# Attention values in column halves, softmax sums by 32 columns of ones in column quarters

## The reference

```
q = (x @ Wq + bq).reshape(Bv, Tv, 16, 8)
k = (x @ Wk + bk).reshape(Bv, Tv, 16, 64)
v = (x @ Wv + bv).reshape(Bv, Tv, 16, 64)
qc = einsum('bthd,dl->bthl', q, Wc)
att = einsum('bthl,bshl->bhts', qc, k) / 8
att = softmax(where(causal, att, -inf), axis=-1)
y = einsum('bhts,bshl->bthl', att, v).reshape(Bv, Tv, 16 * 64)
return y @ Wo + bo
```

## Time and profile before

| | |
|---|---|
| median of 3 runs | 1122.53 us (1118.86 to 1125.27) |
| the profiled execution | 1125.98 us, span 1124.2 us |
| PE busy | 904.0 us, 80% of the span |
| DVE / ACT / POOL busy | 569.0 / 409.8 / 330.6 us |
| value matmuls L1593 | 1280 records, 305.2 us busy |
| the exponentials L820 | 320, 176.6 us |
| sums L770, values L779 out | 47.8 us and 37.5 us |

### The profile page before, as it was taken

How to read it: one execution, slowest core, us unless ns; L and a number is a source line. 1 busy time by engine, 2 the same in 40 slices (tenths; PEclk the granted TensorE clock), 3 DMA queues, 4 the chain that set the end, 5 groups by cost and what they waited for, 6 DMA issues and landing times.

```text
span 1124.2 us, 16448 instructions
## 1 busy us (share of the span) xinstructions
PE 904.0 (80%) x5179; PEld 734.7 (65%) x5179; DVE 569.0 (51%) x1644; ACT 409.8 (36%) x809; POOL 330.6 (29%) x326
## 2 busy tenths in 40 slices
PE   2306599999379889999999799599999937999983
PEld 2204276777237778988886688488888725777663
DVE  8431144444356776665652676267446514444443
ACT  1100122222144555555642455346435522222223
POOL 1736515555400000000000014531000262455551
PEclk9998799999779999999999899799999978999996
DMA  9800225444252021223120021210202102444525
GB/s 344 284 23 28 62 67 151 146 154 147 93 196 58 19 48 29 48 83 106 25 53 10 1 61 48 79 42 21 56 10 48 44 25 58 136 135 149 158 92 190
DMA packets 97475, 99.09 MB, mean 88 GB/s; under 512 B 15225, under 2 KB 82699, under 8 KB 96646
## 3 DMA queue, kind: packets, MB, share of 16 engines
q1 hardware_dynamic: 88198, 85.98, 25.7%
q0 software_dynamic: 9216, 12.33, 3.5%
HBM read 58.62 MB, written 38.60 MB: 86 GB/s over the span
## 4 chain that ended last, share of the span: by engine, by line
PE 56%; DVE 15%; another core or an unknown queue 12%; issue 10%; ACT 3%; DMA 2%; POOL 1%; SPq 1%; DVEq 0%; POOLq 0%; ACTq 0%
PE PS L1593 19%; PE PS L1551 6%; PE PS L1472 5%; PE PS L1576 5%; PE PS L1473 4%; DVE mxp L1167 3%; PE PS L1485 2%; PE PS L1639 2%; PE PS L1493 2%; DVE xs L1149 1%; ACT area_o L741 1%; PE PS L1554 1%; DMA yg<-ybuf 1%; PE PS L1579 1%
## 5 line engine op out<-in xcount | busy, mean ns | idle before, releaser
L1593 PE MATMUL PS<-pT,area_v 128*128 128x256 f32 (+1 forms) x1280 | 305.2, 362 | 4.8 <-ACT area_o L779 4.8
L1167 DVE TENSOR_REDUCE mxp<-PS 128x2 f32<-128x512 f32 (+1 forms) x320 | 197.0, 630 | 139.9 <-PE PS L1551 67.0
L820 ACT ACTIVATE pT<-PS 128x512 f32<-128x512 f32 (+1 forms) x320 | 176.6, 553 | 235.8 <-PE PS L1579 113.9
L1593 PEld LDWEIGHTS PS<-pT,area_v 128*128 128x128 f32 x1280 | 213.9, 194 | 19.0 <-ACT area_o L779 5.1
L657 POOL DMA_INDIRECT ybuf<-area_o,yidx x160 | 155.4, 971 | 162.8 <-DVE area_o L1126 78.4
L643 POOL TENSOR_TENSOR area_o<-area_o,rden 128x512 f32<-128x512 f32 x31 | 39.5, 1273 | 494.0 <-DMA rden<-den 493.7
L1551 PE MATMUL PS<-Kz,Qx 128*128 128x256 f32 (+1 forms) x640 | 168.6, 356 | 18.6 <-DVE mxp L1167 11.3
L613 POOL DMA_INDIRECT xbuf<-xn,sidx x128 | 124.9, 976 | 112.5 <-issue 59.8
L1576 PE MATMUL PS<-Qx,Kz 128*128 128x256 f32 (+1 forms) x640 | 144.0, 307 | 5.4 <-ACT pT L820 2.3
L1551 PEld LDWEIGHTS PS<-Kz,Qx 128*128 128x128 f32 x640 | 113.8, 197 | 40.8 <-DVE mxp L1167 16.0
L1472 PE MATMUL PS<-area_o,area_v 128*128 128x320 f32 x256 | 97.3, 462 | 22.4 <-ACT area_o L741 17.4
(11 more groups left out here) (174 smaller groups left out, 898.5 us busy)
## 6 DMA issues: line engine op xcount, KB each, us to landing
area_v<-xbuf SPq DMA_DIRECT2D x32, 340.0 KB, 3.3
area_v<-in_L_ffn_wg_dram SPq DMA_DIRECT2D x32, 256.0 KB
area_v<-in_L_ffn_wu_dram SPq DMA_DIRECT2D x32, 256.0 KB
area_v<-in_L_ffn_wd_dram SPq DMA_DIRECT2D x64, 128.0 KB
rden<-den SPq DMA_DIRECT2D x248, 32.0 KB
yg<-ybuf SPq DMA_DIRECT2D x24, 256.0 KB, 4.6
qkbuf<-stage SPq DMA_DIRECT2D x24, 256.0 KB, 3.7
xbuf<-Kz SPq DMA_DIRECT2D x4, 1360.0 KB, 12.3
```

The costliest lines, as they stand in the source:

```text
L820: nc.scalar.activation(pT[:, N % 4, 0:w], PS[:, 2 + N % 2, 0:w], ACT.Exp).then_inc(exp_done, 1)
L1167: nc.vector.tensor_reduce(mxp[:, i, c, 2 * hp:2 * hp + 2], PS[:, k % 2, 0:2 * w].rearrange("p (h w) -> p h w", h=2), AX.X, ALU.max).then_i ...
L1593: ins = mm(PS[:, pv_bank(U, a), (p + 1) * TC - w:(p + 1) * TC], value_and_ones(j, h), pT[:, N % 4, a * w:(a + 1) * w], start=(N in UNIT_FI ...
```

## The change

The values lie without ones, 64 columns a head. A step's two value matmuls have 64 stationary columns each and write the lower and the upper half of one bank. After every second step, `p_sums` makes the sums of four heads with 32 columns of ones (from the constants) as stationary operand, into four quarters of another bank; it covers the two head pairs of one key block. `pv_done` rises by 2 there. ACT copies the sums of a unit in one instruction and the values in one. The exponential waits accordingly, and `y_free` counts one a unit. The memset of the ones goes. The mask matmul moves into a function of its own, with the same place in the order.

```diff
-def pv_bank(U, a):
-    return 4 + 2 * (U % 2) + a
+def pv_bank(U):
+    return 5 + 2 * (U % 2)
+def den_bank(U):
+    return 4 + 2 * (U % 2)
...
-        vs = area_v[:].rearrange("p (j c k l) -> p j c k l", j=HT, c=NH // 2, k=3)
+        vs = area_v[:, 0:HT * NH * LAT].rearrange("p (j n) -> p j n", j=HT)
...
-            nc.gpsimd.memset(vs[:, :, :, 1, :], 1.0).then_inc(v_ones, 1)
...
-            def sums(U, p):
+            def sums_out(U):
...
-                for a in range(2):
-                    hh = 2 * p + a
-                    ins = nc.scalar.activation(den[U % 2][RW * hh:RW * hh + RW, :],
-                                               PS[LAT * (1 - a):LAT * (1 - a) + RW, pv_bank(U, a), TC * p:TC * p + TC], ACT.Copy)
-                ins.then_inc(den_ready, 1)
+                nc.scalar.activation(den[U % 2][:], PS[:, den_bank(U), 0:TC], ACT.Copy).then_inc(den_ready, 1)
...
-                lanes = slice(LAT * a, LAT * a + LAT)
-                nc.scalar.activation(yT[lanes, 2 * g:2 * g + 2, c * TC:(c + 1) * TC],
-                                     PS[lanes, pv_bank(U, a), :].rearrange("p (c t) -> p c t", c=2), ACT.Copy).then_inc(y_free, 1)
+                nc.scalar.activation(yT[:, 2 * g:2 * g + 2, c * TC:(c + 1) * TC],
+                                     PS[:, pv_bank(U), :].rearrange("p (c t) -> p c t", c=2), ACT.Copy).then_inc(y_free, 1)
...
                     if N >= 4:
-                        act.wait_ge(pv_done, N - 3)
+                        act.wait_ge(pv_done, N // 2 * 2 - 2)
...
-                dve.wait_ge(den_ready, 2 * U + 2)
+                dve.wait_ge(den_ready, U + 1)
...
                 for a in range(2):
                     h = VISITS[v][1] * HG + 2 * p + a
-                    ins = mm(PS[:, pv_bank(U, a), (p + 1) * TC - w:(p + 1) * TC], value_and_ones(j, h), pT[:, N % 4, a * w:(a + 1) * w],
-                             start=(N in UNIT_FIRST), stop=(j == 0), skip_group_check=True)
-                ins.then_inc(pv_done, 1)
+                    mm(PS[LAT * a:LAT * a + LAT, pv_bank(U), (p + 1) * TC - w:(p + 1) * TC], vs[:, j, h * LAT:(h + 1) * LAT],
+                       pT[:, N % 4, a * w:(a + 1) * w], start=(N in UNIT_FIRST), stop=(j == 0), skip_group_check=True)
+
+            def p_sums(N):
+                v, c, j, p = STEPS[N]
+                w = step_width(N)
+                for hh in range(HG):
+                    ins = mm(PS[RW * hh:RW * hh + RW, den_bank(UNIT_OF[N]), TC - w:TC], cst[:, C_ONE:C_ONE + RW],
+                             pT[:, (N - 1 + hh // 2) % 4, hh % 2 * w:(hh % 2 + 1) * w],
+                             start=(N - 1 in UNIT_FIRST), stop=(j == 0), skip_group_check=True)
+                ins.then_inc(pv_done, 2)
...
+            def one_pv(N):
+                pv(N)
+                if N % 2:
+                    p_sums(N)
```

More of the change, by code:

```diff
@@ L196, in loads, with s_bank @@
     return sum(u <= v and u % 2 == v % 2 for u in LOADED)
-def pv_bank(U, a):
-    return 4 + 2 * (U % 2) + a
+def pv_bank(U):
+    return 5 + 2 * (U % 2)
+def den_bank(U):
+    return 4 + 2 * (U % 2)
+def s_bank(N):
+    return 2 + N % 2
 def score_bank(f):
@@ L298, in program @@
         area_o = sb("area_o", [P, HT * NH * LAT])
-        area_v = sb("area_v", [P, HT * NH // 2 * VP])
+        area_v = sb("area_v", [P, 12 * HC * 512])
         def parts(area, first, *shapes):
@@ L639, in scale @@
                 g, c = VISITS[UNITS[U][0]][1], UNITS[U][1]
-                pool.wait_ge(y_free, 2 * (U + 1))
+                pool.wait_ge(y_free, U + 1)
                 pool.wait_ge(rep_done[U % 2], 16 * 2 * HG * (U // 2 + 1))
@@ L767, in sums, with latents @@
                     act.wait_ge(rep_done[U % 2], 16 * 2 * HG * (U // 2))
-                for a in range(2):
-                    hh = 2 * p + a
-                    ins = nc.scalar.activation(den[U % 2][RW * hh:RW * hh + RW, :],
-                                               PS[LAT * (1 - a):LAT * (1 - a) + RW, pv_bank(U, a), TC * p:TC * p + TC], ACT.Copy)
-                ins.then_inc(den_ready, 1)
-            def latents(U, a):
+                nc.scalar.activation(den[U % 2][:], PS[:, den_bank(U), 0:TC], ACT.Copy).then_inc(den_ready, 1)
+            def latents(U):
                 g, c = VISITS[UNITS[U][0]][1], UNITS[U][1]
                 act.wait_ge(pv_done, UNIT_STEP[U] + 1)
-                lanes = slice(LAT * a, LAT * a + LAT)
-                nc.scalar.activation(yT[lanes, 2 * g:2 * g + 2, c * TC:(c + 1) * TC],
-                                     PS[lanes, pv_bank(U, a), :].rearrange("p (c t) -> p c t", c=2), ACT.Copy).then_inc(y_free, 1)
+                nc.scalar.activation(yT[:, 2 * g:2 * g + 2, c * TC:(c + 1) * TC],
+                                     PS[:, pv_bank(U), :].rearrange("p (c t) -> p c t", c=2), ACT.Copy).then_inc(y_free, 1)
             def unit_out(step, b):
-                for part in range(4):
+                for part, evacuate in enumerate((sums_out, latents)):
                     for U in units_at(step, EVAC + part, b):
[L785 to L788, removed]
+                        evacuate(U)
             def values(b, tiles):
@@ L798, in values @@
                     act.wait_ge(v_ps, HT * b + j + 1)
-                    nc.scalar.activation(vs[:, j, :, 0:3:2, :],
-                                         flat(4 + 2 * (j % 2), 2).rearrange("p (c k l) -> p c k l", k=2, l=LAT),
-                                         ACT.Copy).then_inc(v_a, 1)
+                    nc.scalar.activation(vs[:, j, :], flat(4 + 2 * (j % 2), 2), ACT.Copy).then_inc(v_a, 1)
             def heads(b):
@@ L818, in heads @@
                     if N >= 4:
-                        act.wait_ge(pv_done, N - 3)
-                    nc.scalar.activation(pT[:, N % 4, 0:w], PS[:, 2 + N % 2, 0:w], ACT.Exp).then_inc(exp_done, 1)
+                        act.wait_ge(pv_done, N // 2 * 2 - 2)
+                    nc.scalar.activation(pT[:, N % 4, 0:w], PS[:, s_bank(N), 0:w], ACT.Exp).then_inc(exp_done, 1)
                     unit_out(N, b)
@@ L1260, in last_norms @@
                 dve.wait_ge(rep_ps, 1)
-                dve.wait_ge(y_free, 2 * (U_LAST + 1))
+                dve.wait_ge(y_free, U_LAST + 1)
                 y = yT[:, 2 * g:2 * g + 2, c * TC:(c + 1) * TC]
-                tt(y, y, PS[:, pv_bank(U_LAST, 0), :].rearrange("p (c t) -> p c t", c=2), ALU.mult).then_inc(last_norm, 1)
+                tt(y, y, PS[:, pv_bank(U_LAST), :].rearrange("p (c t) -> p c t", c=2), ALU.mult).then_inc(last_norm, 1)
             def last_part():
@@ L1398, in last_part @@
                 pe.wait_ge(exp_done, len(STEPS))
-                pe.wait_ge(y_free, 2 * U_LAST)
+                pe.wait_ge(y_free, U_LAST)
                 gate_up_rows(1, 0)
@@ L1423, in replicate @@
                 pe.wait_ge(rec_ready, U_LAST + 1)
-                pe.wait_ge(y_free, 2 * (U_LAST + 1))
+                pe.wait_ge(y_free, U_LAST + 1)
                 for p in range(2):
@@ L1427, in replicate @@
                         row = RW * (2 * p + a)
[L1428 removed]
+                        ins = mm(PS[LAT * a:LAT * a + LAT, pv_bank(U_LAST), TC * p:TC * p + TC],
                                  ident[:, row:row + 1].broadcast_to([P, LAT]), den[U_LAST % 2][:],
@@ L1575, in s_cols, with s_mask @@
                 for a in range(2):
-                    ins = mm(PS[:, 2 + N % 2, a * w:(a + 1) * w], Kz[v % 2][:, 2 * p + a, j * P:(j + 1) * P],
+                    ins = mm(PS[:, s_bank(N), a * w:(a + 1) * w], Kz[v % 2][:, 2 * p + a, j * P:(j + 1) * P],
                              Qx[v % 2][:, t1 - w:t1], start=(a == 0), stop=N not in DIAG, skip_group_check=True)
[L1578 to L1581, removed]
+                if N not in DIAG:
+                    ins.then_inc(st_ready, 1)
+            def s_mask(N):
+                w = step_width(N)
+                mm(PS[:, s_bank(N), 0:2 * w].rearrange("p (h w) -> p h w", h=2)[:, :, 0:P], causS[:],
+                   identb[:].unsqueeze(1).broadcast_to([P, 2, P]), start=False, stop=True, skip_group_check=True).then_inc(st_ready, 1)
             def pv(N):
@@ L1588, in pv @@
                 if N in UNIT_FIRST and U >= 2:
-                    pe.wait_ge(y_free, 2 * (U - 1))
+                    pe.wait_ge(y_free, U - 1)
                 pe.wait_ge(exp_done, N + 1)
@@ L1600, in heads @@
                     s_cols(N)
+                    if N in DIAG:
+                        s_mask(N)
                     if N - LAG in steps:
-                        pv(N - LAG)
+                        one_pv(N - LAG)
                     for k in rows_at(N):
@@ L1605, in heads @@
                 for N in steps[-LAG:]:
-                    pv(N)
+                    one_pv(N)
+            def one_pv(N):
+                pv(N)
+                if N % 2:
+                    p_sums(N)
             def out_rows(b):
@@ L1688, in _ @@
             pe.wait_ge(v_a, HT)
-            pe.wait_ge(v_ones, 1)
             heads(0)
```

(2 more changed lines are left out.)

6 lines of the change are left out of this document (1 added, 5 removed).

## The result

The changed kernel takes 1184.67 us (median of 4 runs, 1184.34 to 1186.17), the kernel before 1121.09 us (median of 4; a fourth run of 1119.64 us has joined the three above). The ratio is 1.0557, with a 95% interval of 1.0536 to 1.0579: slower. Forecast were 1178 us and 1140 to 1230.

What follows compares the result with a forecast made beforehand. PE was taken to bound the attention loop. The profiled 1126.0 us plus 63 us on PE less 8 us absorbed gave 1181, less 3.5 to the median: 1178 us, range 1140 to 1230.

Steps and rivals of the forecast that it cites:

- The shorter matmuls: Value and sum matmuls on PE run side by side, 6 slots instead of 8 per pair of steps, saving 62 us.
- four abreast: The sums' 32-column records on PE run in all four quarters at once, taking 2 slots of 0.216 us per wide pair.
- The change of shape: On PE, five changes of column width per pair, each about 0.09 us of waiting plus the weight load, 0.78 us together.
- The sum: PE in the attention loop: 63 us more from shape changes less saved slots, 8 us absorbed by slack, net +55 us.
- The parts costed at nothing: Off PE's path: ACT's 55 us less work, POOL's memset removed, the exponential's later wait (bounds 0 and 15 us), taken at 0.
- Hidden changes of shape: Rival: PE's weight loads are pulled ahead at changes of shape, so the gain stands, about 1068 us; chance 0.07.
- Two abreast: Rival: the sums' quarters on PE run only two at once, so sums take 4 slots, 1240 us; chance 0.08.
- The clock: Rival: PE's waits lower its clock; with a fifth of the loop at 1.2 GHz, near 1270 us; chance 0.04.
- 16 us more were estimated: For the sums' four column tiles on PE, a loss like the skill's 2.38 of 3 would add 16 us to the sum.

Runs made afterwards that it cites:

- the sums twice: The changed kernel with the sums of each pair of steps done twice in a row into the same place: 112.8 us over the kernel before (1144.53 us).
- the faster chip: The changed kernel and the kernel before, both unaltered, run again on another chip: 1089.81 against 1030.52 us, ratio 1.0574.
- the tiny matmul: Changed kernel, values of two steps together, an extra 8-column matmul between them: 49.6 us over the kernel before with 64 stationary columns, 76.2 us with 128.
- the two and the four steps at a time: Changed kernel with values of two steps in one go: 40.2 us over the kernel before; of four: 53.6 us, with a third row bank 15.2 us.

## Why the prediction was right

*The shorter matmuls.* Both halves and all four quarters run at once; the value taken for four abreast, of which no row stood, was right to a few ns (the sums twice). It was carried over from the halves, as was the halving of the load down to 32 columns; both came true, but no row before the result supported them.

*The change of shape.* Forecast were five per pair at 0.14, 0.12, 0.19, 0.14 and 0.19 us. In the timeline values start at 562.22 and the row item at 562.80, 0.58 us later: two slots (0.43), the open load of 64 columns ahead of the first (0.05) and 0.10 us until the array is free. The row item's own load then takes another 0.10 us in the open (the first record of such a matmul lasts 0.385 us, behind a matmul of its own shape 0.281): some 0.20 us for this change. The first value's own change is 0.10 + 0.05 = 0.15 us. The change from 64 to 32 columns was taken as 0.12 us without a row: from 563.47 to 564.05 it is again 0.58 us, so again 0.10 us until the array is free, and 0.02 us for the open load (first record 0.403 against 0.379 us). That makes 0.12 us. The five are 0.82 us in all, forecast 0.78.

*The sum.* On the faster chip values and sums with the changes into their shapes take 255.4 us against 248.7, all else in the loop 329.3 against 275.2. By the prediction's figures the first should grow by 160 x (2 x 0.14 + 0.12) - 62 = 2 us, measured 6.7; the second by 320 x 0.19 = 61, measured 54.1, since waits took some up. On the first chip they grew by 3.1 us (258.4 against 255.3) and 56.6 us (346.2 against 289.6). The net growth was forecast as 55 us and came as 60 to 61. The 5 to 6 us are the price of the change, taken too low: with 0.82 us instead of 0.78 the 160 pairs cost 131 instead of 125 us, less 62 us of slots 69 instead of 63. Of these 69 us, 8 to 9 were absorbed, as forecast (some more if the clock below took its 3 to 4). 1181 us for a profiled execution became 1186.2.

*The parts costed at nothing* (ACT's copies, the memset, the exponential's wait, the clock) were small: ACT's copies and the exponential's wait within some 5 us each, by the experiments. The memset has no run of its own; the loop starts 0.7 us earlier without it.

*The rivals.* Hidden changes of shape: out, by the tiny matmul and by the timeline. Two abreast: out. The clock: 0.97 in the loop in both on the first chip, but 0.99 before and 0.98 after on the faster one. Added up over the traces, 41.0 us of the changed kernel's loop lie at the 1.2 GHz level against 33.8, on the faster chip 20.5 against 13.7. That is 7 us more each time and costs at most 3 to 4 of the 60 us (an estimate), where the rival had set a fifth of the loop (its 1270 us stands there without a working). The rule of the Trainium skill, TensorEngine Tiling (Array Packing), Key Properties, that changing the tiling mode drains TensorE, held in each of these traces: no weight load of a new shape starts before the matmul ahead of it has streamed, and then 0.09 us more. What passes in these 0.09 us no run shows. The measured speedup of 2.38 for three column tiles that the Trainium skill states (TensorE: Matmul & The Clock Gate, Part 3), and from which 16 us more were estimated, doesn't carry over: with 256 moving f32 columns four tiles lose nothing between bursts of the same shape (0.432 us for eight records more).

What was not foreseen is how little room a remedy has. The expectations for the two and the four steps at a time priced changes of shape as if they could be batched freely; batching clumps the row items, and the gain goes into waits for DVE and a lower clock.

## What to carry to other kernels

Matmuls of half or a quarter of the columns do run side by side, but each change between column widths costs the wait until the array is free and an open weight load, here 0.12 to 0.20 us. So count the changes before the slots: a group must save more than its two or three changes cost, here 0.35 to 0.47 us or about two slots of 256 f32 columns. And when work is regrouped for this, run the same regrouping on the old kernel as a control, since the new order may cost more than the changes that it saves.

## What was not expected of the hardware

The open load of 128 bf16 columns costs far less than that of 128 f32 columns: behind the tiny matmul's load at 503.06 its matmul's record lasts 0.18 us, with 64 columns and a hidden load 0.17. The same kernel took 1121 us in the first runs and 1126, 1032 and 1031 us on three later chips. Between the first chip and the last, it takes 346.6 against 301.0 us ahead of the loop, 232.7 against 207.0 behind it (stages that move experts' weights and rows; what slows them is not traced) and, in the loop, 544.9 against 523.9. Of these last 21 us, 13 are idle time of PE (38.1 against 25.3), and 20 us more at the 1.2 GHz level account for at most another 10.
